# Bias and level rows laid out by dimension for merged operand loads in attention, and a three-level split on ScalarE and VectorE

## The reference

```python
# layer 0
q = (x @ Wq.T + bq).reshape(B, S, H, Dh).transpose(0, 2, 1, 3)   # k, v alike
scores = einsum('bhqd,bhkd->bhqk', q, k) / sqrt(Dh) + slopes * (k_pos - q_pos)
y = einsum('bhqk,bhkd->bhqd', softmax(where(causal, scores, -inf)), v)
# layer 1: two maps, att1 from q1, k1 and att2 from q2, k2; their softmaxes are combined with a
# learned factor lambda, applied to v, normalized per head and projected
```

## Time and profile before

| | us |
|---|---|
| median of three runs (lowest, highest) | 6779.74 (6776.26, 6789.61) |
| profiled execution | 6790.24 |
| its span | 6788.4 |
| busy in it: PE, DVE, ACT, POOL | 5217.8, 3361.2, 2483.8, 1576.2 |
| `bp` units, first to last | 771 to 852 |
| `ba`, first load to last scores | 904 to 2022 |
| `ep` units, first to last | 3540 to 3697 |
| `ea`, first load to last scores | 3756 to 5944 |

### The profile page before, as it was taken

The page is one execution under the profiler, slowest core; times in us unless marked ns, Lnnn a source line. Parts: engine busy times, 40 slices in busy tenths (PEclk is TensorE's granted clock), DMA queues, the critical chain, the costliest instruction groups (busy, mean ns, idle before and its releaser), DMA issues. The chain is left out here.

```text
span 6788.4 us, 95548 instructions
## 1 busy us (share of the span) xinstructions
PE 5217.8 (77%) x30112; PEld 2794.8 (41%) x30112; DVE 3361.2 (50%) x5679; ACT 2483.8 (37%) x4942; POOL 1576.2 (23%) x1276
## 2 busy tenths in 40 slices
PE   6466448888787466489968688878888888976997
PEld 3355223333235355247953233323333333343696
DVE  7511646666544821311148566756666666533111
ACT  2011106555561011122211266656655655612221
POOL 2388300000101178433324000000000000002332
PEclk9688769999898678789989699989998999988998
DMA  2376431112203177507955211111111111011498
GB/s 93 98 150 138 132 111 41 42 42 59 64 21 116 31 169 149 137 2 243 330 174 163 64 34 35 55 43 35 40 53 41 34 43 53 15 63 35 146 325 272
DMA packets 454298, 660.17 MB, mean 97 GB/s; under 512 B 97984, under 2 KB 308992, under 8 KB 448672
## 3 DMA queue, kind: packets, MB, share of 16 engines
q1 hardware_dynamic: 383232, 544.50, 25.6%
q0 software_dynamic: 70656, 110.44, 8.0%
HBM read 489.33 MB, written 164.20 MB: 96 GB/s over the span
## 5 line engine op out<-in xcount | busy, mean ns | idle before, releaser
L1642 DVE TENSOR_REDUCE ea_mx<-ea_psA 128x1 f32<-128x1024 f32 (+7 forms) x1280 | 1317.6, 1061 | 697.5 <-PE ea_psA L1507 491.4
L1624 ACT ACTIVATE ea_pr<-ea_psB 128x512 f32<-128x512 f32 (+3 forms) x2560 | 1229.7, 535 | 934.6 <-PE ea_psB L1529 514.5
L1504 PE MATMUL ea_psA<-ea_kx,ea_qx 99*128 99x512 bf16 (+3 forms) x2560 | 730.0, 363 | 285.4 <-DMA ea_kx<-in_c_k 256.0
L1642 DVE TENSOR_REDUCE ba_mx<-ba_psA 128x1 f32<-128x1024 f32 (+7 forms) x640 | 657.4, 1061 | 381.5 <-PE ba_psA L1507 282.5
L1529 PE MATMUL ea_psB<-ea_qx,ea_kx 99*128 99x512 bf16 (+3 forms) x2560 | 782.7, 354 | 29.0 <-issue 21.0
L1624 ACT ACTIVATE ba_pr<-ba_psB 128x512 f32<-128x512 f32 (+3 forms) x1280 | 610.7, 535 | 494.8 <-PE ba_psB L1529 260.3
L1544 PE MATMUL ea_psO<-ea_pr,ea_vx 128*32 128x512 f32 (+3 forms) x5120 | 612.2, 551 | 1.9 <-ACT ea_pr L1624 0.4
L1504 PE MATMUL ba_psA<-ba_kx,ba_qx 108*128 108x512 bf16 (+3 forms) x1280 | 371.7, 369 | 198.2 <-DMA ba_kx<-in_c_k 181.3
L1504 PEld LDWEIGHTS ea_psA<-ea_kx,ea_qx 99*128 99x128 bf16 x2560 | 217.9, 100 | 695.1 <-issue 383.4
L1476 POOL DMA_DIRECT2D ea_qx<-ea_mT x192 | 106.0, 559 | 1546.3 <-DVE ea_mT L1664 1521.9
L1529 PEld LDWEIGHTS ea_psB<-ea_qx,ea_kx 99*128 99x128 bf16 x2560 | 242.3, 99 | 501.0 <-ACT ea_pr L1624 315.2
(11 more groups left out here) (522 smaller groups left out, 8297.0 us busy)
## 6 DMA issues: line engine op xcount, KB each, us to landing
de_wg<-in_L_rg SPq DMA_DIRECT2D x64, 512.0 KB
de_wu<-in_L_ru SPq DMA_DIRECT2D x64, 512.0 KB
de_wd<-in_L_rd SPq DMA_DIRECT2D x64, 512.0 KB
fe_wg<-in_L_rg SPq DMA_DIRECT2D x64, 512.0 KB
fe_wu<-in_L_ru SPq DMA_DIRECT2D x64, 512.0 KB
fe_wd<-in_L_rd SPq DMA_DIRECT2D x64, 512.0 KB
ae_w<-in_L_w SPq DMA_DIRECT2D x64, 384.0 KB, 3.7
ce_w<-in_L_w SPq DMA_DIRECT2D x64, 384.0 KB
```

What stands on the lines that cost most here:

```text
L1504: last = nc.tensor.matmul(psA[:, slot, at:at + n], qx[0:KB, s, hh, t * P:(t + 1) * P], kx[0:KB, s, hh, k:k + n], start=True, stop=not diag)
L1624: nc.scalar.activation(pr[:, j % 2, hh, off:BLK], psB[:, exp_slot(n, s), off:BLK], ACT.Exp).then_inc(s_exp, 1)
L1642: v.tensor_reduce(out, src, AX.X, ALU.max).then_inc(s_ar, 1)
```

## The change

In `project_phase` ScalarE writes t32 and then, with a second activation from the same PSUM buffer, level 0 in bf16. VectorE does the subtraction, the cast to level 1 and the subtraction for level 2, which was GpSimd's. GpSimd has no work in the phase. ScalarE now waits for the store that used a `lev` buffer, and for `s_lo` in place of `s_r`.

The columns of the projection matrices are reordered ahead of the launch, so that a row of `lvq` and `lvk` holds one dimension, and the four maps of a step lie in four consecutive rows for each dimension. One DMA then loads all four maps for one n: rows of 16 KB, three DMAs for q and three for k per step. For layer 1 the two maps' rows alternate (`of_map`), so that one tensor of 1024 rows per level holds what were two of 512. The bias rows, 9 in `ba` and none in `ea`, come in one DMA each for q and k, laid out in the same way. The rows of ones in `kx` are the last three and are loaded once, at the start of the phase, for each of the two buffers. The matmuls for the maxima run over `KA` rows, without those three (105 or 96), the scores over `KB` (108 or 99). In SyncE's order all queries and `vx` take the place of half 0, all keys that of half 1. The rest of the edits follows from these (a semaphore per buffer and not per half, the sizes of constants).

```diff
@@ -1159,10 +1159,13 @@
 
                 def scaled(n, b, i, k, m, half, first):
                     act.wait_ge(s_mm, n + 1)
-                    after(act, s_r, n, 2, first)
+                    after(act, s_lo, n, 2, first)
                     a = {} if vbias is None else {"bias": bias[:, 2 * m + half:2 * m + half + 1]}
                     f = ACT.Copy if vbias is None else ACT.Identity
-                    nc.scalar.activation(t32[:, k % 2, :], ps[:, k % 2, :], f, scale=mats[m][2],
+                    nc.scalar.activation(t32[:, k % 2, :], ps[:, k % 2, :], f, scale=mats[m][2], **a)
+
+                    act.wait_ge(s_out[k % NL], ((b * QB + i) * (nu // NL) + k // NL) * 16)
+                    nc.scalar.activation(lev[:, k % NL, 0], ps[:, k % 2, :], f, scale=mats[m][2],
                                          **a).then_inc(s_t, 1)
                 blocks(act, scaled)
 
@@ -1187,14 +1190,11 @@
                 def split(n, b, i, k, m, half, first):
                     u, v = k % 2, k % NL
                     dve.wait_ge(s_t, n + 1)
-
-                    dve.wait_ge(s_out[v], ((b * QB + i) * (nu // NL) + k // NL) * 16)
-                    nc.vector.tensor_copy(lev[:, v, 0], t32[:, u, :]).then_inc(s_c, 1)
+                    nc.vector.tensor_tensor(res[:, u, :], t32[:, u, :], lev[:, v, 0], ALU.subtract).then_inc(s_c, 1)
                     dve.wait_ge(s_c, base + n * 2 + 1)
-                    after(dve, s_lo, n, 2, first)
-                    nc.vector.tensor_tensor(res[:, u, :], t32[:, u, :], lev[:, v, 0], ALU.subtract).then_inc(s_c, 1)
+                    nc.vector.tensor_copy(lev[:, v, 1], res[:, u, :]).then_inc(s_c, 1)
                     dve.wait_ge(s_c, base + n * 2 + 2)
-                    nc.vector.tensor_copy(lev[:, v, 1], res[:, u, :]).then_inc(s_r, 1)
+                    nc.vector.tensor_tensor(lev[:, v, 2], res[:, u, :], lev[:, v, 1], ALU.subtract).then_inc(s_lo, 1)
                 blocks(dve, split)
                 for t in range(NT):
                     u = t % 2
@@ -1207,14 +1207,6 @@
                     else:
                         nc.vector.tensor_tensor(vs[:, u, :, 0:VH], src, vb[:].rearrange("p (h v) -> p h v", h=NHEAD),
                                                 ALU.add).then_inc(s_vs, 1)
-
-            @block.gpsimd
-            def _(pool):
-                def rest(n, b, i, k, m, half, first):
-                    pool.wait_ge(s_r, n + 1)
-                    nc.gpsimd.tensor_tensor(lev[:, k % NL, 2], res[:, k % 2, :], lev[:, k % NL, 1],
-                                            ALU.subtract).then_inc(s_lo, 1)
-                blocks(pool, rest)
 
 
 UNITS = [(Q, kt) for Q in range(QB) for kt in range((Q + 1) * BLK // P)]
...
@@ -1298,14 +1290,14 @@
 FIRST_MAXIMA = [e for i in range(CUT) for e in [("A", (0, i))] + [(k, (0, KIND_LAST.index(i))) for k in "LM" if i in KIND_LAST]]
 
 
-def attention_phase(nc, name, D, C, lvq, lvk, vd, yT, sums, sgn, maps, qc, kc, F, MR, s_m, st0):
+def attention_phase(nc, name, D, C, lvq, lvk, vd, yT, sums, sgn, maps, qc, kc, ones, F, s_m, st0):
     two = maps == 2
     steps = B * NHEAD * maps // HV
-    KB = F + KP
-    shared = qc.shape[0] == F
+    KA, KB = KP + F, KP + F + 3
+    MR = KA
     VCOL = vd.shape[-1] // KT
     YR = P // maps
-    nld = 14
+    nld = 8 if F else 6
     SR = DH if maps == 1 else VW - 1
     SC = HV * S // P
     with Scope(nc, name) as sc:
@@ -1323,7 +1315,7 @@
         psA = sc.ps("psA", [P, NRING, 2 * BLK])
         psO = sc.ps("psO", [P, BLK])
 
-        s_ld = [[sc.sem(f"ld{s}{g}") for g in range(2)] for s in range(2)]
+        s_ld, s_one = [sc.sem(f"ld{s}") for s in range(2)], sc.sem("one")
         s_v = [sc.sem(f"v{s}") for s in range(2)]
         s_yo = [sc.sem(f"yo{s}") for s in range(2)]
 
@@ -1393,28 +1385,27 @@
 
             @block.sync
             def _(sp):
-                def load(st, s, *groups):
-                    for g in groups:
-                        if two:
-                            lq, lk, r0, own = lvq[g], lvk[g], st * (2 * DH), slice(g, HV, 2)
-                        else:
-                            lq, lk, r0, own = lvq[0], lvk[0], st * (HV * DH) + g * 2 * DH, slice(2 * g, 2 * g + 2)
-                        at = F
-                        for n in (3, 2, 1):
-                            for h, hh in enumerate(range(HV)[own]):
-                                rows = ds(r0 + h * DH, DH)
-                                sp.dma_start(qx[at:at + n * DH, s, hh, :],
-                                             lq[3 - n, rows, :].unsqueeze(0).broadcast_to((n, DH, S))).then_inc(s_ld[s][g], 16)
-                                sp.dma_start(kx[at:at + n * DH, s, hh, :], lk[0:n, rows, :]).then_inc(s_ld[s][g], 16)
-                            at += n * DH
-                        for dst, src in ((qx, qc), (kx, kc)):
-                            sp.dma_start(dst[0:F, s, own, :],
-                                         src.unsqueeze(1).broadcast_to((F, 2, S)) if shared else
-                                         src[ds((st * HV + 2 * g) * F, 2 * F), :].rearrange("(h f) s -> f h s", h=2)
-                                         ).then_inc(s_ld[s][g], 16)
-                    if 0 in groups:
-                        sp.dma_start(vx[:, s].rearrange("p k c -> p (k c)"),
-                                     vd[ds(st, 1)].rearrange("g p c -> p (g c)")).then_inc(s_v[s], 16)
+                def load_queries(st, s):
+                    at = 0
+                    for n in (3, 2, 1):
+                        src = lvq[3 - n, ds(st * HV * DH, HV * DH), :].rearrange("(d h) s -> d (h s)", h=HV)
+                        sp.dma_start(qx[at:at + n * DH, s].rearrange("p h s -> p (h s)"),
+                                     src.unsqueeze(0).broadcast_to((n, DH, HV * S))).then_inc(s_ld[s], 16)
+                        at += n * DH
+                    if F:
+                        sp.dma_start(qx[KP:KA, s].rearrange("p h s -> p (h s)"), qc[ds(st * F, F), :]).then_inc(s_ld[s], 16)
+                    sp.dma_start(vx[:, s].rearrange("p k c -> p (k c)"),
+                                 vd[ds(st, 1)].rearrange("g p c -> p (g c)")).then_inc(s_v[s], 16)
+
+                def load_keys(st, s):
+                    at = 0
+                    for n in (3, 2, 1):
+                        sp.dma_start(kx[at:at + n * DH, s].rearrange("p h s -> p (h s)"),
+                                     lvk[0:n, ds(st * HV * DH, HV * DH), :].rearrange("l (d h) s -> l d (h s)", h=HV)
+                                     ).then_inc(s_ld[s], 16)
+                        at += n * DH
+                    if F:
+                        sp.dma_start(kx[KP:KA, s].rearrange("p h s -> p (h s)"), kc[ds(st * F, F), :]).then_inc(s_ld[s], 16)
 
                 def sums_out(st, s, use):
 
@@ -1447,16 +1438,19 @@
                     if nxt:
                         if prev:
                             sp.wait_ge(s_av, st * NU)
-                        load(st + 1, 1 - s, 0)
+                        load_queries(st + 1, 1 - s)
                     if prev:
                         inverses_in(st - 1, 1 - s, use + s - 1)
                     if nxt:
-                        load(st + 1, 1 - s, 1)
+                        load_keys(st + 1, 1 - s)
                     if prev:
                         for Q in range(QB):
                             result_out(st - 1, 1 - s, Q)
 
-                load(0, 0, 0, 1)
+                load_queries(0, 0)
+                load_keys(0, 0)
+                for u in range(2):
+                    sp.dma_start(kx[KA:KB, u], ones.unsqueeze(1).broadcast_to((3, HV, S))).then_inc(s_one, 16)
 
                 steps_of(sp, body)
                 end, s = steps - 1, (steps - 1) % 2
@@ -1501,8 +1495,8 @@
                         [(heads[0], 0, k0, BLK), (heads[0], BLK, k0 + BLK, m - BLK)]
                     for hh, at, k, n in runs:
                         diag = k + n == (t + 1) * P
-                        last = nc.tensor.matmul(psA[:, slot, at:at + n], qx[0:KB, s, hh, t * P:(t + 1) * P],
-                                                kx[0:KB, s, hh, k:k + n], start=True, stop=not diag)
+                        last = nc.tensor.matmul(psA[:, slot, at:at + n], qx[0:KA, s, hh, t * P:(t + 1) * P],
+                                                kx[0:KA, s, hh, k:k + n], start=True, stop=not diag)
                         if diag:
                             last = nc.tensor.matmul(psA[:, slot, at + n - P:at + n], C["identb"], C["maskA"],
                                                     start=False, stop=True)
...
@@ -1939,16 +1932,15 @@
     for st in range(steps):
         for hh in range(HV):
             for l, s in enumerate(three_levels(np.float32(SLOPES[st % (NHEAD // HV) * HV + hh]))):
-                r = 3 * l if l == 0 else 3 * l + 3
+                r = 3 * l
                 q[st, hh, r], k[st, hh, r] = -(j // BLK) * BLK, s
```

(28 more changed lines are left out.)

## The result

The changed kernel takes 6956.8 us (median; 6955.1 to 6960.8) against 6782.7 us before in the same comparison: a ratio of 1.0257, with an interval of 1.0240 to 1.0275. It is 174 us slower, where 64 us less was forecast (6716), and outside the range of 6630 to 6775.

What follows compares the result with a forecast made beforehand. VectorE was taken to bound the projections, loads on three or two DMA engines the attention steps. Projections - 51, constants - 18 and starts + 5 gave - 64 us: 6716 us, range 6630 to 6775.

Steps and rivals of the forecast that it cites:

- The bound and its cause: Attention steps wait for operand loads whose outermost copies confine them to three or two engines; waits 325 us plus two starts.
- The split: Projections: without GpSimd, VectorE stays the bound at 1.83 us per unit, for 2.37 and 2.39; together 51 us less.
- A longer piece gains nothing: 0: Attention loads: rows of 16 KB for 4 KB leave bytes, engines and the rate per engine unchanged; effect 0.
- The unexplained 11 us of a step: Attention load chain: latencies and shared stretches that the new order might change, + 20 to - 80 us; taken as 0.
- The constants and starts: Attention: dropped constant loads in `ea` save 18 us; the first waits, taking in `vx` and ones, cost 5 us.
- (b): Rival, attention loads: 16 KB pieces move slower, 0.30 us more per piece, + 436 us, so 7150; chance 5%.
- (c): Rival, key loads: levels 4 MB apart in `lvk` collide in memory, + 462 us, so 7180; chance 4%.
- the estimate of 7000: Key loads: by the Trainium skill's rates at 2 MB and 4 MB pitch, keys take 34 us and not 21.
- (d): Rival, nothing net: the split runs at 2.1 us per unit and a worse order eats the rest, 6766 to 6793; 7%.
- (a): Rival, attention loads: merged loads use all 16 engines, waits vanish, starts fall some 35 us each, 6340; chance 7%.

Runs made afterwards that it cites:

- the cut kernel: Changed kernel with each load of 3 or 2 copies cut in two by dimension, pieces still 16 KB: 6691.6 us, ratio 0.9867 to the kernel before.
- (7): Probe loads ahead of the fast kernel's phases: 2 copies of 32 rows, 32 partitions apart, in four loads with 4 KB rows: at most 24 us.

## Why the prediction was wrong

- **The bound and its cause: right.** Three and two engines carried the loads, each step waited for them, and turning the outermost dimension, with the same bytes and pieces, took away all the waits between the starts and some 610 us of the changed kernel.
- **The split: right.** Forecast -51 us; measured -46, and 56 between profiled spans. The unit took 1.79 us for 1.83, the second subtraction 0.69 as assumed, and VectorE stayed the bound, as forecast, with TensorE close behind.
- **"A longer piece gains nothing: 0": this step failed.** The term measured +230 us: with pieces of 4 KB in the same layout and order the kernel is 56 us under the kernel before, with pieces of 16 KB 174 above it. Bytes and engines stayed, as I had them, but not the 25.3 GB/s of each engine. I read the `vx` row, 51 GB/s on two engines, as a property of piece length. But where the engines write counts too: the partitions in flight at one time. Before the change, the first and third engine already wrote 32 apart, and the earlier trace rows showed 77 GB/s for three: with 4 KB rows a lead, once gained, parts them. With 16 KB rows the same lead in rows is four times the bytes, and so what was a passing collision stayed through most of a load of three copies. No row of before shows it at 16 KB, and the `vx` row could not bound it, since its engines write other partitions.
- **The unexplained 11 us of a step: "I take 0".** For the new order this held (one map per load, new order: 6721 us). But I left the 11 us unexplained, and some 1.3 of them were this collision: pieces of 16 KB cut by dimension beat pieces of 4 KB by 30 us in 22 steps (6692 against 6721).
- **The constants and starts:** forecast -13 us together, measured -10 (6721 against 6731), within the intervals of both.
- **The rivals.** (b) had the right sign and twice the size (+436), for a wrong reason: there is no fixed price per piece, since 16 KB pieces win in the cut kernel. (c) is refuted, and the estimate of 7000 beside it: the levels of `lvk` lay 4 MB apart in every variant of the changed kernel, and three engines that read them moved 78 GB/s. (d) was wrong in its slow unit of 2.1 us. (a) was wrong for the change as made. Its price for what it named, 6340 against 6337, was partly luck: the two starts fell by 42 us and not by 70, and it left out that without the waits TensorE is busy 52 us less (5165.6 for 5217.8), at a mean granted clock of 0.90 for 0.88.
- **The new wait for `rec`** I had not seen at all. I had the inverses behind the first half of the loads, and treated what delays that half as a matter of the key wait alone. In `ea` it has a second customer, the matmul of line 1551 (1545 after), at fixed slots of the step, and its wait is 73 us of the 196.

What stays open is how the lead arises that parts two engines with short rows. That they part is shown by the packets of (7), where the slow ones end at the 21st of 128.

## What to carry to other kernels

Read the DMA share first: 0.19 or 0.12 of 16 means three or two engines, and the outermost dimension of the load is the thing to turn, not the number or size of loads. Where several engines write one load, look at how far apart their partitions are: here two at a distance of 32 shared one engine's rate, and rows of 16 KB kept them there. A change that shortens issue only helps where a profile shows transfers waiting for issue.

## What the runs showed of the hardware that I had not expected

Two DMA engines that wrote rows of 16 KB to partitions 32 apart moved 29 GB/s together, and 54 at a distance of 64, on an idle core. Three engines moved 80 GB/s in steps of 8 partitions and 52 in steps of 16. The same collision, with rows of 4 KB, cost 2 us of 12 where rows of 16 KB cost 8.5.
